# Attention heads normalised feature-major through DRAM, and 32-column TensorE tiles in phase one, in a two-layer kernel

## What is computed

```python
x = layernorm(x + mamba_and_mlp(x))      # state space mixer, 4 heads of 64, state 128; gated MLP of 512
x = layernorm(x + top2_of_8_experts(x))  # dense 128x128 experts, softmax router
# attention, 16 heads of 8, with a relative sinusoidal bias
qkv = xn @ w_qkv + b_qkv
attn = softmax(q @ k.T * 8**-0.5 + bias[head, i - j])
out = (attn @ v).transpose(0, 2, 1, 3).reshape(b, t, 128)
x = layernorm(x + out @ w_out + b_out)
# 8 experts, top 2, capacity 512 tokens each, in the order of the tokens
x = layernorm(x + moe(x))                # silu(a) * g, hidden 192
```

## Time and profile before

| | |
|---|---|
| median of 3 runs | 1428.94 us (1427.57 to 1433.79) |
| profiled execution, own time | 1423.66 us |
| its span, first to last instruction | 1421.9 us |
| mean granted TensorE clock | 0.970 of full |

### The profile page before, as it was taken

One profiled execution on the slowest core, in us unless ns is written; L12 is line 12 of the kernel. 1 busy time (PEld: TensorE's weight loads), 2 busy tenths in 40 slices (PEclk: granted clock), 3 DMA queues, 4 the chain that ended last, 5 costly groups with the idle time before them and its releaser, 6 DMA issues. The chain is left out here.

```text
span 1421.9 us, 37391 instructions
## 1 busy us (share of the span) xinstructions
PE 1285.9 (90%) x15528; PEld 702.5 (49%) x15528; DVE 1103.2 (78%) x2228; ACT 905.4 (64%) x1746; POOL 277.2 (19%) x411
## 2 busy tenths in 40 slices
PE   5998898888887978999999999999999999994896
PEld 2556455553644523555555454555545554542452
DVE  6776887779685687999998989989899889943123
ACT  5655345427432403988898888888888888883142
POOL 2221121121112004000000110601105111034472
PEclk9999999999999988999999999999999999997899
DMA  5080000200104803011110211112110100001135
GB/s 138 1 223 15 1 1 15 108 1 0 75 35 90 181 18 147 3 26 25 25 26 3 45 25 25 41 18 45 25 24 23 29 4 3 4 6 38 38 112 183
DMA packets 50762, 65.63 MB, mean 46 GB/s; under 512 B 12030, under 2 KB 38209, under 8 KB 48754
## 3 DMA queue, kind: packets, MB, share of 16 engines
q1 hardware_dynamic: 47522, 59.00, 16.2%
q0 software_dynamic: 3072, 4.25, 0.9%
HBM read 33.24 MB, written 32.03 MB: 46 GB/s over the span
## 5 line engine op out<-in xcount | busy, mean ns | idle before, releaser
L1425 ACT ACTIVATE space<-ps 128x512 f32<-128x512 f32 x1024 | 604.6, 598 | 108.0 <-PE ps L607 60.9
L607 PE MATMUL ps<-space 96*32 96x512 bf16 (+3 forms) x8688 | 640.0, 378 | 32.6 <-DVE space L1923 14.4
L2072 DVE TENSOR_REDUCE smax<-ps 128x1 f32<-128x1024 f32 x512 | 614.8, 1222 | 60.4 <-PE ps L607 36.1
L607 PEld LDWEIGHTS ps<-space 96*32 96x32 bf16 (+3 forms) x8688 | 267.5, 99 | 315.4 <-issue 48.3
L971 PE MATMUL ps<-space 128*32 128x256 f32 x4096 | 317.4, 379 | 0.0
L971 PEld LDWEIGHTS ps<-space 128*32 128x32 f32 x4096 | 134.4, 111 | 88.8 <-issue 5.2
L1529 POOL TENSOR_SCALAR eps_sum<-mv 128x4 f32<-128x4 f32 x32 | 7.3, 229 | 584.7 <-DVEq L1788 584.3
L1283 ACT ACTIVATE btok<-ps 128x128 f32<-128x128 f32 x32 | 8.9, 278 | 123.4 <-issue 103.5
L607 PE MATMUL ps<-w_exp,xnT 128*128 128x512 f32 x128 | 64.5, 628 | 12.3 <-DVE x L2017 12.3
L2017 DVE SCALAR_TENSOR_TENSOR x<-ps,gsel,x 128x128 f32<-128x128 f32 x256 | 69.1, 342 | 8.1 <-PE ps L607 7.7
L607 PE MATMUL ps<-ones,ident 128*128 128x512 bf16 x228 | 59.4, 421 | 17.4 <-POOLq L1632 12.3
(11 more groups left out here) (248 smaller groups left out, 1417.6 us busy)
## 6 DMA issues: line engine op xcount, KB each, us to landing
q_rows<-space SPq DMA_DIRECT2D x24, 256.0 KB, 2.4
k_rows<-space SPq DMA_DIRECT2D x24, 256.0 KB, 2.8
space<-k_rows SPq DMA_DIRECT2D x16, 384.0 KB, 5.2
space<-q_rows SPq DMA_DIRECT2D x16, 384.0 KB, 6.8
expert_out<-x_all SPq DMA_DIRECT2D x2, 2048.0 KB, 20.2
space<-expert_out SPq DMA_DIRECT2D x4, 1024.0 KB, 8.8
v_rows<-space SPq DMA_DIRECT2D x4, 668.0 KB, 3.7
space<-v_rows SPq DMA_DIRECT2D x4, 668.0 KB, 6.9
```

Source lines behind the costliest of these rows:

```text
L607: return nc.tensor.matmul(out, lhsT, rhs, start=first, stop=last)
L1425: nc.scalar.activation(prob[:, QUAD * (step % PROB_SETS) + unit % QUAD, :], bank(STB + unit % 2), ACT.Exp)\
L2072: v.tensor_reduce(smax[:, N % 2, i:i + 1], ps[:, b0:b0 + 2, :].rearrange("p k n -> p (k n)"), AX.X, ALU.max).then_inc(S.s_max, 1)
```

## The change

**Heads stay feature-major.** `pv_transpose`, `outputs`, `heads_turned` and `evac_heads` go. SyncE stores `pv_sb` (256 KB) to DRAM after each run but the last and reads the 32 feature rows back into one of two tiles, `o_num` (`heads_move`). Once the last quad of a half is done, SyncE gathers the 16 denominator rows as 128 rows of 64 numbers (`denominators_gathered`), VectorE takes their reciprocals in two pieces at pairs 13 and 14 of the run after (`inverse`), and at the start of the next run SyncE stores them and reads them back, each row repeated over the 8 features of its head, into `o_den` (`denominators_spread`). GpSimd multiplies the two tiles into `xnT` (`heads_scaled`). For the last batch VectorE multiplies, and the last quad of the second half goes the old way round through TensorE (`last_heads`).

**Nine columns for the values.** `pv_burst` uses 9 weight columns per head, where it had 32; the values' rows shrink from 167 to 144 columns per tile.

**32-column tiles** in `step_sizes`, `mix_out` and `route`: each 128-column product becomes four 32-column ones. In `chunk_out` the four 64-column products now come ahead of the two 128-column ones.

**GpSimd** adds the output bias of all four batches ahead of its loop. (In the kernel before, each batch's addition stood at the head of that batch's iteration.)

```diff
-TURN_AT, SHIFT_AT = 2, 6
-OUTPUTS_AT, EVAC_SHIFT_AT = 5, 11
+SHIFT_AT = 6
+EVAC_SHIFT_AT = 11
+INVERSE_AT = 13, 14
...
+        inverted_after = {(b, H): HALVES * b + HALVES - 2 + H for b in range(B) for H in range(2)}
+        inverted_after[B - 1, 1] = HALVES * B - 3
...
+            def heads_move(N):
...
+                sp.wait_ge(S.pv_evac, N + 1)
+                if b >= 1:
+                    sp.wait_ge(S.heads_ready, 2 * b - 1 + qh)
+                sp.dma_start(head_sums[qh, q], pv_sb[:]).then_inc(S.sums_stored, 16)
+                sp.wait_ge(S.sums_stored, sums_stored(N))
...
+                sp.dma_start(o_num[QUAD * HD * q:QUAD * HD * (q + 1), half(qh)], rows[:, 0:HD, :]).then_inc(S.heads_moved, 16)
...
             for N in range(B * HALVES):
                 shift_rows_back(N)
+                for (b, H), at in inverted_after.items():
+                    if at == N - 2:
+                        denominators_spread(b, H)
...
+                if N >= 1:
+                    heads_move(N - 1)
+                for (b, H), at in inverted_after.items():
+                    if at == N - 1:
+                        denominators_gathered(b, H)
+            denominators_spread(B - 1, 0)
...
                 for i in range(NT):
-                    last = mm(bank(TRB)[:, SSM_HEADS * i:SSM_HEADS * i + SSM_HEADS], tile(xinT, i),
-                              w_in[:, 768:768 + SSM_HEADS])
+                    for c in range(COL_GROUPS):
+                        last = mm(bank(TRB)[quadrant(c), SSM_HEADS * i:SSM_HEADS * i + SSM_HEADS], columns(tile(xinT, i), c),
+                                  w_in[:, 768:768 + SSM_HEADS])
...
                     for j in range(2):
-                        mm(tile(bank(MIX_BANK[H]), i), tile(zg[:, j], n), w_out[:, j], j == 0, j == 1)
+                        for c in range(COL_GROUPS):
+                            mm(tile(bank(MIX_BANK[H]), i)[quadrant(c)], columns(tile(zg[:, j], n), c), w_out[:, j], j == 0, j == 1)
...
-                    last = mm(bank(to)[:, E * i:E * i + E], tile(xnT, i), w[:])
+                    for c in range(COL_GROUPS):
+                        last = mm(bank(to)[quadrant(c), E * i:E * i + E], columns(tile(xnT, i), c), w[:])
...
-                if kt == TURN_AT and N > 0:
-                    pv_transpose(N - 1)
...
             def evac_pv(N):
                 act.wait_ge(S.pv_done, NT * (N + 1))
                 if N > 0:
-                    act.wait_ge(S.pvT_psum, N)
+                    act.wait_ge(S.sums_stored, sums_stored(N - 1))
...
+            def heads_scaled(b, H):
+
+                if H == 0:
+                    pool.wait_ge(*((S.route_psum, B + b) if b >= 1 else (S.v_psum, 2 * B)))
+                pool.wait_ge(S.heads_moved, 16 * (inverted_after[b, H] + 1))
+                pool.wait_ge(S.den_spread, 16 * (inverse_turn[b, H] + 1))
+                g.tensor_tensor(xnT[:, half(H)], o_num[:, half(H)], o_den[:, half(H)], ALU.mult).then_inc(S.heads_ready, 1)
...
+            def inverse(b, H, part):
...
+                dve.wait_ge(S.den_loaded, 16 * (inverse_turn[b, H] + 1))
...
+                v.reciprocal(den_c[rows, cols], den_c[rows, cols]).then_inc(S.den_inverse, 1)
```

More of the change, by code:

```diff
@@ L135, in build @@
         v_rows = dram("v_rows", [B, P, NT * VROW])
+        head_sums = dram("head_sums", [2, QUADS, P, HALF])
+        den_rows = [dram(f"den_rows{H}", [P, DEN_COLS]) for H in range(2)]
         shift_rows = dram("shift_rows", [SHIFT_PARTS * 16, P], BF16)
@@ L334, in build @@
         v_back = S.v_back0, S.v_back1
+        LAST_TURNED, LAST_RECIP, LAST_READY, LAST_BACK, LAST_IN = range(1, 6)
         rows_back = S.rows_back0, S.rows_back1, S.rows_back2, S.rows_back3
@@ L399, in spare_bank, with sums_stored, inverted @@
             return 6 + (n + 1) % 2
+        def sums_stored(N):
+            return 16 * (N + 1 + sum(at < N for at in inverted_after.values()))
+        inverted_after = {(b, H): HALVES * b + HALVES - 2 + H for b in range(B) for H in range(2)}
+        inverted_after[B - 1, 1] = HALVES * B - 3
+        inverse_turn = {bH: i for i, bH in enumerate(sorted(inverted_after, key=inverted_after.get))}
+        def inverted(b, H):
+            return P if (b, H) != (B - 1, 1) else P - LAST_ROWS
         def rest_bank(e):
@@ L699, in chunk_out, with out @@
                 pe.wait_ge(S.yt_ready, NT * b + c + 1)
+                def out(j):
+                    return tile(bank(YB), 2 * j + c % 2)
                 for j in range(2):
-                    out = tile(bank(YB), 2 * j + c % 2)
                     for h in range(2):
-                        mm(out[SSM_DIM * h:SSM_DIM * h + SSM_DIM], xdt[:, c % 2, 2 * j + h], Wm[:, c % 2, 2 * j + h], True, False)
-                    last = mm(out, ytok[:, c % 2, 2 * j:2 * j + 2].rearrange("p h d -> p (h d)"), ident[:], False, True)
+                        nc.tensor.matmul(out(j)[SSM_DIM * h:SSM_DIM * h + SSM_DIM], xdt[:, c % 2, 2 * j + h], Wm[:, c % 2, 2 * j + h],
+                                         start=j == 0, stop=False, skip_group_check=True)
+                for j in range(2):
+                    last = nc.tensor.matmul(out(j), ytok[:, c % 2, 2 * j:2 * j + 2].rearrange("p h d -> p (h d)"), ident[:],
+                                            start=False, stop=True, skip_group_check=True)
                 last.then_inc(S.y_psum, 1)
@@ L1060, in _ @@
                     pv_burst(step, part)
-            pv_transpose(HALVES * B - 1)
             pe.wait_ge(S.s_max, 16 * HALVES * B)
             pe.wait_ge(S.p_ready, 32 * HALVES * B)
-            for H in range(2):
-                heads_turned(B - 1, H, H)
-            for H in range(2):
-                heads_projected(B - 1, H, 2 + H)
-            pe.wait_ge(S.oT_sb, 2 * B)
+            heads_projected(B - 1, 0, 2)
+            evacuated(HALVES * B)
+            transposes(lambda i: tile(pv_sb, i), bank(run_bank(HALVES * B - 1)), S.last_heads_step)
+            pe.wait_ge(S.last_heads_step, LAST_READY)
+            transposes(lambda i: x2[:, i, :], bank(1), S.last_heads_step)
+            pe.wait_ge(S.last_heads_step, LAST_IN)
+            heads_projected(B - 1, 1, 3)
             keep_clock(5, 16)
@@ L1431, in _ @@
             evac_pv(HALVES * B - 1)
-            for H in range(2):
-                evac_heads(B - 1, H, H)
+            act.wait_ge(S.route_psum, 2 * B - 1)
+            act.wait_ge(S.last_heads_step, LAST_BACK)
+            nc.scalar.activation(xnT[P - LAST_ROWS:P, half(1)], bank(1)[P - LAST_ROWS:P], ACT.Copy).then_inc(S.last_heads_step, 1)
             for H in range(2):
@@ L1687, in _ @@
                 bias_rows(b)
+            for b in range(B):
                 for k in range(TOPK):
                     row_numbers(b, k)
+                if b + 1 < B:
+                    for H in range(2):
+                        heads_scaled(b, H)
                 for H in range(2):
@@ L2294, in _ @@
                     N, i = (pair - 16 - LEAD) // 16, (pair - 16 - LEAD) % 16
-                    if i == OUTPUTS_AT and N > 0:
-                        outputs(N - 1)
                     if i == EVAC_SHIFT_AT and N < HALVES * B - 1:
                         evac_shift(N + 1)
+                    for (b, H), at in inverted_after.items():
+                        if at == N - 1 and i in INVERSE_AT:
+                            inverse(b, H, INVERSE_AT.index(i))
                     if N >= HALVES:
                         after_attention(N // HALVES - 1, N % HALVES, i)
-            outputs(HALVES * B - 1)
+            for H in range(2):
+                heads_scaled(B - 1, H)
+            last_heads()
             dve.wait_ge(S.slot_ready, B - 1)
```

116 lines of the change are left out of this document (65 added, 51 removed).

## The result

The changed kernel takes 1388.7 us (median of 4 runs, 1385.2 to 1392.1), the kernel before 1428.3 beside it: a ratio of 0.973 with a 95% interval of 0.970 to 0.975. In a later series the same kernel took 1387.2 us, ratio 0.973 (0.971 to 0.975). So it is faster by about 39 us; 43 were forecast.

The account below looks back on a forecast made before the run. TensorE's own time bounds attention; phase one is a chain between engines. Terms 22.0 + 6.6 - 1 + 1.5 + 14 = 43.1 us, so 1428.94 - 43.1 = 1386 us, range 1373 to 1404.

Parts of the forecast that it names:

- The transposes of the sums: In attention, one group of four transposes goes from each of runs 1 to 31, 0.71 us each: 22.0 us.
- turning the heads back: In attention, three runs lose the work of turning a batch's heads, 2.19 us each: 6.6 us.
- Nine columns at nothing: In attention, nine value columns in place of 32 change no time, as the same 256 columns stream through.
- Reciprocals: In attention, VectorE's reciprocals for six halves could stop TensorE for 0 to 4.2 us; a loss of 1 us taken.
- SyncE at nothing: In attention, SyncE's new stores and loads fit in the 11.4 us ahead of the shift's first DMA: no cost.
- no TensorE wait for the shift beyond before's: Sign in attention: TensorE waits no longer for the shift's DMAs than in the kernel before.
- SyncE late for the shift: Rival in attention: DMAs just before lengthen the shift's store, 0.5 us per run, 15.5 in all, 1401 us; chance 0.09.
- The tail: After attention, the second half's inverse root starts earlier, as the first half needs no transposes: 1.5 us (0 to 3).
- Phase one: Before attention, some 31 us less TensorE work in projections, router, step sizes and chunks; 14 us of it gained (0 to 31).
- The two waits named: In phase one, VectorE's waits for `mix_out` (7.5 us) and the router (5.4 us), forecast to fall by 6.5 and 3.9.
- some of it will show as another wait: Last step for phase one: its gains sum to 14.6 us, part returns as other waits, so 14 us.
- The clock rival: Phase one, with less TensorE work, spends twice as long at 1.2 GHz; its 14 us go, 1400 us; chance 0.06.

Follow-up runs that it names:

- run 8: Not an experiment: one of the stretches of attention between copies of the sums, in which a batch's heads were turned back; 23.96 us before, 21.07 in the changed kernel.
- the four stores: The changed kernel with four more 256 KB stores to DRAM per run on SyncE, each waited for, ahead of the store of the sums: 1467.8 us, ratio 1.032.
- order only: The kernel before with the new order of products in `chunk_out` and nothing else: 1422.3 us, ratio 0.998.
- run 12: Not an experiment: a stretch of the changed kernel's attention between copies of the sums, 23.68 us long, whose shift store took 3.52 us instead of 1.39.

## Why the prediction was right

**The transposes of the sums (22.0) and turning the heads back (6.6): right.** 0.70 us per run, 2.89 us in run 8 (0.70 of it the transposes). In the changed kernel attention is 23.9 us under before, 24.0 in its second profile. With the shift half a step earlier it is 28.0 and 27.8 under before; 28.6 less 1 were forecast. Attention takes 719.2 to 721.3 us in the four profiles with the old heads, so these figures hold to some 2 us.

**Nine columns at nothing: right,** half steps of 1.31 us. **Reciprocals (1): small, as forecast**, and not measured apart; run 8, which has such a pair of them, takes 21.07 us like an ordinary run. The cover that the text named, landing by pair 13, is real: six pairs earlier costs some 8 us of attention.

**SyncE at nothing: right for its queue, wrong for what hangs on it.** This is the one term that was clearly missed, by some 4 us, and the sign "no TensorE wait for the shift beyond before's" failed: 10.4 us for 3.8. The queue is free 7.3 us ahead of the shift, and what goes well beyond that costs attention time, as the four stores show. The rival "SyncE late for the shift" had the place right; its cause, DMAs just before that lengthen the store, doesn't act in the changed kernel, where the last of them is issued some 3 us or more ahead and ordinary runs keep their 1.39 us. It is real, though: with four more stores, where the gap is mostly under 0.1 us, it adds some 1 us to the store, also in the ten runs without an instruction packet near. In the changed kernel ten stores are 0.4 to 2.1 us late, each beside an instruction packet, and cost 4 to 5 us in all where the rival had 15.5. Late stores aren't much more frequent with the new heads: the four profiles of kernels with the old ones have 8 to 10 of them, with 3.8 to 5.7 us of waits for the shift's rows on the weight loads. The two profiles of the changed kernel have ten each, with 10.4 and 9.9. Why they cost more there is open.

**The tail (1.5): 2.1 from copy to root, 2.9 in the tail as a whole;** but the tail of profiles with the same code varies from 133.1 to 136.2, 134.3 on the mean of seven, and that of the kernel before and of "order only" is 136.4 and 135.8. So some 2 us.

**Phase one: the mechanism right; the size, 14 us, at the upper side of what was measured.** TensorE was freed of what was forecast: 477.9 busy us against 446.9 in the profile with as much time at the low clock (54.6 us, the one with the inverse early), 31.0 us:

```profile
0.00:555.00 555.00, 446.86 (x3451) 250.91 (x3451) 426.93 (x1241) 242.72 (x583) 118.33 (x179) 0.95 0.24 67
```

The two waits named fell by 5.3 + 5.1 = 10.4 us in the trace, as forecast. What came of it on the whole: 9.7 us measured apart, 7.5 + 3.0 = 10.5 from its two parts, 15 as the whole less the heads, 12.0 and 8.5 from the profiles at equal time at the low clock. With intervals of 3 to 5 us on the first three these agree with each other, and 14 isn't ruled out. By term: the tiles 7.5 us (5 to 10) for 6.5 + 3.9 = 10.4, the chunks 3.0 (0 to 5) for 3.2. If something was mis-sized, it is the last step, "some of it will show as another wait", taken at 0.6. The sign "phase one ending near 552" came out at 560.2 and 556.7, 554.2 on the line above at the low-clock time of before.

The rule of the Trainium skill weighed there ("TensorEngine Tiling (Array Packing)", Instruction Overhead: some 60 cycles for each matmul) would have let the router gain 0.25 us; it gained 1.13, with 64 records in 0.72 us, as the row of 62 records had it.

**The clock rival** didn't come true: over all executions the mean clock is that of before. The clock did distort the profile after by some 4 to 9 us, which a single pair of traces would have put down to phase one's code. The rival's price rests on a slip: 57 us more at 1.2 GHz cost products at most 28 us more, not 43. Its result of 14 us is what 57 us would cost at the measured 0.24 us each, by luck.

**The sum.** Forecast 43.1 us; 39 there, with an interval of some 3 to 4 us on either side. The late shifts account for the 4 that are missing: with the shift half a step earlier the gain is 44.3 and 43.5 us. How close the other terms come together is in part luck, since phase one was forecast "between 0 and 31" and is known to some 3 us only.

## What to carry to other kernels

A DMA round trip that an engine needs in every round should have slack for its slow landings, not for its median: here 1.4 us as a rule, 1.8 to 3.5 ten times in an execution, and half a step of lead was worth 4 us. Moving a step earlier helps only until it passes the work that frees its buffer, and then turns a stall that comes and goes into a fixed one. Compare stages of two profiles at the same time spent at the low clock, or measure the parts apart: one pair of traces here showed 6 us in a stage that gave 10 to 15.

## What the runs showed of the hardware

A 16 KB instruction packet takes 0.9 to 1.6 us on a DMA engine, and the ten 8 KB stores of the trace after that had one near were 0.4 to 2.1 us late; in run 12, 45 of the store's packets started within 0.2 us, and three as the instruction packet ended. The same store issued within 0.1 us behind a 64 KB load took 2.4 us, where it takes 1.4 with 7 us between. One kernel's executions spend 65 and 85 us at 1.2 GHz in the same 560 us stage, at 0.24 us of its length for each. Extra products without a reader in the gaps didn't change that by more than executions differ.
